# Second attention of a transformer stack: stored relative terms narrowed and stored in two partition halves, split stacks gathered twice

## The reference, cut to what matters

```python
# H = 16 heads, D = 8 channels per head, M = 128, S = 512 tokens, dist_emb has 2*M - 1 = 255 rows
scores = jnp.einsum('bhqd,bhkd->bhqk', q, k)
dist_idx = pos_l - pos_r + M - 1                 # below 0 it wraps, beyond the table it is clipped
pos_emb = dist_emb[dist_idx]
rel_q = jnp.einsum('bhld,lrd->bhlr', q, pos_emb)
rel_k = jnp.einsum('bhrd,lrd->bhlr', k, pos_emb)
probs = jax.nn.softmax((scores + rel_q + rel_k) / sqrt(D), axis=-1)
ctx = jnp.einsum('bhqk,bhkd->bhqd', probs, v)
```

## Time and profile before

| what | us |
|---|---|
| median of 3 runs | 4911.35 |
| profiled execution, its own time | 4912.15 |
| its span in the trace | 4910.4 |
| first phase b1 in the trace, 32 units | 2243 to 3059 |
| second phase b2 in the trace, 32 units | 3059 to 3974 |

### The profile page before, as it was taken

One profiled execution on the slowest core, in us unless ns is written; L12 is line 12 of the kernel. 1 busy time (PEld: TensorE's weight loads), 2 busy tenths in 40 slices (PEclk: granted clock), 3 DMA queues, 4 the chain that ended last, 5 costly groups with the idle time before them and its releaser, 6 DMA issues.

```text
span 4910.4 us, 102424 instructions
## 1 busy us (share of the span) xinstructions
PE 3915.1 (80%) x31924; PEld 2380.9 (48%) x31924; DVE 2889.9 (59%) x6305; ACT 2635.3 (54%) x6550; POOL 1689.6 (34%) x1383
## 2 busy tenths in 40 slices
PE   2999999999488888734666565999999945888886
PEld 1555555554255555522222222677777723555554
DVE  2555555555577777543444443566666665777775
ACT  1555555554367777523333333566666624777774
POOL 0000000000588888523222222111111116878774
PEclk9999999999799999965555555999999977999998
DMA  3222222221111111027999999777777711111111
GB/s 118 87 78 78 78 78 80 81 78 53 49 25 23 27 27 23 17 71 293 380 381 385 380 381 369 269 262 260 248 272 250 256 43 52 25 26 25 25 23 32
DMA packets 374686, 701.06 MB, mean 143 GB/s; under 512 B 54180, under 2 KB 161016, under 8 KB 374568
## 3 DMA queue, kind: packets, MB, share of 16 engines
q1 hardware_dynamic: 330536, 565.25, 33.6%
q0 software_dynamic: 44032, 134.30, 7.4%
HBM read 336.53 MB, written 314.64 MB: 133 GB/s over the span
## 4 chain that ended last, share of the span: by engine, by line
PE 51%; DMA 13%; DVE 10%; issue 9%; POOL 7%; ACT 4%; SPq 2%; DVEq 1%; POOLq 0%; ACTq 0%
DMA rel_k<-b_stage_k 12%; PE ps L332 5%; PE ps L1465 5%; PE ps L340 5%; PE ps L351 5%; PE ps L1474 5%; PE ps L1456 3%; PE ps L1485 3%; DVE f_rs L1028 2%; POOL f_rn L758 2%; PE ps L866 2%; DVE f_rc L1025 2%; POOL f_rot L756 2%; PE ps L1357 2%; DVE b_stage_k L1381 2%
## 5 line engine op out<-in xcount | busy, mean ns | idle before, releaser
L1381 DVE COPY b_stage_k<-ps 128x640 f32<-128x640 f32 (+2 forms) x512 | 359.1, 722 | 469.6 <-DMA rel_k<-b_stage_k 410.3
L430 ACT ACTIVATE a_p<-a_s,a_min 128x512 f32<-128x512 f32 x512 | 366.0, 715 | 470.3 <-DVE a_min L474 470.3
L1378 ACT ACTIVATE b_stage_q<-ps 128x640 f32<-128x640 f32 (+2 forms) x512 | 316.0, 624 | 505.4 <-PE ps L1360 388.0
L474 DVE CUSTOM_DVE_ANT_0 a_s<-ps,a_table 128x512 f32<-128x512 f32 x512 | 333.5, 689 | 374.5 <-PE ps L332 371.9
L1539 ACT ACTIVATE c_p<-c_s,c_min 128x512 f32<-128x512 f32 x512 | 370.2, 723 | 290.7 <-PE ps L1474 180.3
L1357 PE MATMUL ps<-b_e,b_st_k 48*128 48x512 bf16 (+1 forms) x512 | 305.9, 597 | 261.1 <-DVE b_stage_k L1381 261.1
L1574 DVE CUSTOM_DVE_ANT_0 c_s<-ps,c_rq 128x512 f32<-128x512 f32 x512 | 352.8, 689 | 200.8 <-PE ps L1465 188.1
L188 POOL COPY y<-ln_rows 128x512 f32 x32 | 19.9, 621 | 1304.8 <-DVE ln_rows L180 1304.8
L949 ACT ACTIVATE f_p<-f_s,f_min 128x128 f32<-128x128 f32 x1024 | 396.3, 390 | 89.1 <-DVE f_min L1014 88.7
L756 POOL TENSOR_TENSOR f_rot<-f_rc,f_rs 128x1024 f32<-128x1024 f32 x128 | 302.9, 2367 | 255.6 <-DVE f_rs L1028 255.3
L758 POOL TENSOR_TENSOR f_rn<-f_ss,f_power 128x16 f32<-128x16 f32 x128 | 373.8, 2920 | 14.9 <-DVE f_ss L1037 1.4
(11 more groups left out here) (171 smaller groups left out, 9194.5 us busy)
## 6 DMA issues: line engine op xcount, KB each, us to landing
rel_q<-b_stage_q SPq DMA_DIRECT2D x64, 1280.0 KB, 7.8
rel_k<-b_stage_k SPq DMA_DIRECT2D x64, 1280.0 KB, 7.7
c_rq<-rel_q SPq DMA_DIRECT2D x64, 1024.0 KB, 7.7
c_rk<-rel_k POOLq DMA_DIRECT2D x64, 1024.0 KB, 11.9
a_table<-skew_bias SPq DMA_DIRECT2D x64, 896.0 KB, 4.6
f_vb<-f_v SPq DMA_DIRECT2D x256, 128.0 KB, 2.4
rel_k<-b_stage_k SPq DMA_DIRECT2D x32, 1024.0 KB, 9.5
rel_q<-b_stage_q SPq DMA_DIRECT2D x32, 1024.0 KB, 5.3
```

The lines of the kernel that those rows point to most:

```text
L430: nc.scalar.activation(a_p[:, lt % 2, h, :], a_s[:, lt % 2, h, :], ACT.Exp, bias=a_min[:, lt % 2, h:h + 1], scale=-1.0, accum_out=a_sum[:, ...
L1381: moves_b1(dve, 1, lambda out, src: nc.vector.tensor_copy(out, src))
```

## The change

The tensor stack_qk and its stores, waits and semaphore go. The window of q and k loses its last column (and for q's lt 0 the first 127, for k's last lt the last 128), and the columns left out are read in b2 from where the same distance stands 255 columns on, in a second DMA. The window lies at the start of its PSUM banks, so products are split 512 columns after lo. Each store of a slot is split into two DMAs, one of partitions 0 to 63 and one of 64 to 127, each 64 columns narrower than the window. In b2 POOL's queue gathers the stacks from split_qk in 12 DMAs of 32 KB in place of one DMA of 384 KB.

```diff
-    b_st_stored = [starting("b_st_stored0", 32), starting("b_st_stored1", 32)]
     def span(n, t):
-        return (P * max(0, t - 1), WIN) if n == 0 else (0, min(WIN, P * (t + 3)))
+        if n == 0:
+            return (P - 1 if t == 0 else P * (t - 1), WIN - 1)
+        return (0, WIN - 1 - P if t == LT - 1 else min(WIN - 1, P * (t + 3)))
+
+    def reads(n, t):
+        if n == 0:
+            return [(0, P, DIST_B), (P, SEQ, 0)] if t == 0 else [(P * (t - 1), SEQ, 0)]
+        return [(0, SEQ - P, 0), (SEQ - P, SEQ, -DIST_B)] if t == LT - 1 else [(0, min(SEQ, P * (t + 2)), 0)]
...
     def sync_b1(sp):
         def step(u, q, i):
-            hold(sp, b_st_loaded[q], i * 192 + 192)
-            for n in range(2):
-                sp.dma_start(stack_dram[u, n], b_st[n][:, q, :, :]).then_inc(b_st_stored[q], 16)
             for lt in range(LT):
                 for n in range(2):
                     lo, hi = span(n, lt)
                     hold(sp, b_rel_moved[n], u * 16 + (lt * QB + QB + 2))
-                    dst = bass.AP(rel_dram[n].tensor, ..., [[WIN, P], [P * WIN, QB], [1, hi - lo]])
-                    sp.dma_start(dst, b_stage[n][:, lt % 2, :, lo:hi]).then_inc(b_rel_stored[n][lt % 2], 16)
+                    for g in range(2):
+                        f, t = (lo + P // 2, hi) if g == 0 else (lo, hi - P // 2)
+                        dst = bass.AP(rel_dram[n].tensor, ... + (lt * HB * P * WIN + g * (P // 2) * WIN + f),
+                                      [[WIN, P // 2], [P * WIN, QB], [1, t - f]])
+                        sp.dma_start(dst, b_stage[n][g * (P // 2):(g + 1) * (P // 2), lt % 2, :, f:t]
+                                     ).then_inc(b_rel_stored[n][lt % 2], 16)
...
     def tensor_b1(pe):
-                        last = nc.tensor.matmul(ps[:, bank, lo:min(hi, 512)], w, b_e[:, n, at + lo:at + min(hi, 512)],
-                        if hi > 512:
-                            last = nc.tensor.matmul(ps[:, bank + 1, 0:hi - 512], w, b_e[:, n, at + 512:at + hi],
+                        mid = min(hi, lo + SEQ)
+                        last = nc.tensor.matmul(ps[:, bank, 0:mid - lo], w, b_e[:, n, at + lo:at + mid], start=True, stop=True)
+                        if hi > mid:
+                            last = nc.tensor.matmul(ps[:, bank + 1, 0:hi - mid], w, b_e[:, n, at + mid:at + hi],
...
     def pool_b2(pool):
             hold(pool, c_scored, u * TILES + 16)
-            pool.dma_start(c_st[:, q, :, :, :].rearrange("p n h t -> p n (h t)"),
-                           stack_dram[u].rearrange("n p h t -> p n (h t)")).then_inc(c_loaded[q], 16)
+            for n in range(2):
+                for g in range(6):
+                    at = (n * 3 + SPLIT_ORDER[n][g]) * (P * SEQ)
+                    src = bass.AP(split_dram.tensor, ..., [[SEQ, DB], [DB * SEQ, QB], [1, SEQ]])
+                    pool.dma_start(c_st[DB * g:DB * g + DB, q, n, :, :], src).then_inc(c_loaded[q], 16)
             for rt in range(LT):
+                for f, t, by in reads(1, rt):
+                    src = bass.AP(rel_dram[1].tensor, ... + (rt * HB * P * WIN + P - 1 + f + by),
+                                  [[WIN - 1, P], [P * WIN, QB], [1, t - f]])
+                    pool.dma_start(c_rk[:, q, rt, :, f:t], src).then_inc(c_loaded[q], 16)
```

More of the change, by code:

```diff
@@ L1113, in program @@
     split_dram = nc.dram_tensor("split_qk", [BATCH, 2, 3, P, SEQ], BF16).ap()
-    stack_dram = nc.dram_tensor("stack_qk", [UNITS_B, 2, STACK, QB, SEQ], BF16).ap()
     rel_dram = [nc.dram_tensor("rel_q", [BATCH, LT, HB, P, WIN], F32).ap(),
@@ L1297, in program @@
     b_st_loaded = [sem("b_st_loaded0"), sem("b_st_loaded1")]
-    b_st_stored = [starting("b_st_stored0", 32), starting("b_st_stored1", 32)]
     b_rel_full = [starting("b_relq_full", 32), starting("b_relk_full", 32)]
     b_rel_moved = [starting("b_relq_moved", 2), starting("b_relk_moved", 2)]
-    b_rel_stored = [[starting("b_relq_stored0", 16), starting("b_relq_stored1", 16)],
-                    [starting("b_relk_stored0", 16), starting("b_relk_stored1", 16)]]
+    b_rel_stored = [[starting("b_relq_stored0", 32), starting("b_relq_stored1", 32)],
+                    [starting("b_relk_stored0", 32), starting("b_relk_stored1", 32)]]
     def span(n, t):
-        return (P * max(0, t - 1), WIN) if n == 0 else (0, min(WIN, P * (t + 3)))
+        if n == 0:
[5 more added lines that the diff above has]
+        return [(0, SEQ - P, 0), (SEQ - P, SEQ, -DIST_B)] if t == LT - 1 else [(0, min(SEQ, P * (t + 2)), 0)]
     def unit_loop(eng, step):
@@ L1315, in step @@
         def step(u, q, i):
-            hold(pool, b_st_stored[q], i * 32 + 32)
             hold(pool, b_rel_full[0], u * 16 + 16)
@@ L1335, in step @@
                     hold(sp, b_rel_moved[n], u * 16 + (lt * QB + QB + 2))
-                    dst = bass.AP(rel_dram[n].tensor,
-                                  (u // QB) * (LT * HB * P * WIN) + (u % QB) * (QB * P * WIN) + (lt * HB * P * WIN + lo),
-                                  [[WIN, P], [P * WIN, QB], [1, hi - lo]])
-                    sp.dma_start(dst, b_stage[n][:, lt % 2, :, lo:hi]).then_inc(b_rel_stored[n][lt % 2], 16)
+                    for g in range(2):
+                        f, t = (lo + P // 2, hi) if g == 0 else (lo, hi - P // 2)
+                        dst = bass.AP(rel_dram[n].tensor, (u // QB) * (LT * HB * P * WIN) + (u % QB) * (QB * P * WIN)
+                                      + (lt * HB * P * WIN + g * (P // 2) * WIN + f), [[WIN, P // 2], [P * WIN, QB], [1, t - f]])
+                        sp.dma_start(dst, b_stage[n][g * (P // 2):(g + 1) * (P // 2), lt % 2, :, f:t]
+                                     ).then_inc(b_rel_stored[n][lt % 2], 16)
         unit_loop(sp, step)
         for n in range(2):
-            sp.wait_ge(b_st_stored[n], 32 + 32 * (UNITS_B // 2))
             for q in range(2):
-                sp.wait_ge(b_rel_stored[n][q], 16 + 16 * (UNITS_B * 2))
+                sp.wait_ge(b_rel_stored[n][q], 32 + 32 * (UNITS_B * 2))
     def tensor_b1(pe):
@@ L1356, in step @@
                         lo, hi = span(n, lt)
-                        last = nc.tensor.matmul(ps[:, bank, lo:min(hi, 512)], w, b_e[:, n, at + lo:at + min(hi, 512)],
-                                                start=True, stop=True)
-                        if hi > 512:
-                            last = nc.tensor.matmul(ps[:, bank + 1, 0:hi - 512], w, b_e[:, n, at + 512:at + hi],
+                        mid = min(hi, lo + SEQ)
+                        last = nc.tensor.matmul(ps[:, bank, 0:mid - lo], w, b_e[:, n, at + lo:at + mid], start=True, stop=True)
+                        if hi > mid:
+                            last = nc.tensor.matmul(ps[:, bank + 1, 0:hi - mid], w, b_e[:, n, at + mid:at + hi],
                                                     start=True, stop=True)
@@ L1367, in step @@
             for lt in range(LT):
-                eng.wait_ge(b_rel_stored[n][lt % 2], u * 32 + (16 * (lt // 2) + 16))
+                eng.wait_ge(b_rel_stored[n][lt % 2], u * 64 + (32 * (lt // 2) + 32))
                 for h in range(QB):
@@ L1372, in step @@
                     lo, hi = span(n, lt)
-                    move(b_stage[n][:, lt % 2, h, lo:hi], ps[:, bank:bank + 2, :].rearrange("p b n -> p (b n)")[:, lo:hi])\
+                    move(b_stage[n][:, lt % 2, h, lo:hi], ps[:, bank:bank + 2, :].rearrange("p b n -> p (b n)")[:, 0:hi - lo])\
                         .then_inc(b_rel_moved[n], 1)
@@ L1424, in step @@
             hold(pool, c_scored, u * TILES + 16)
-            pool.dma_start(c_st[:, q, :, :, :].rearrange("p n h t -> p n (h t)"),
-                           stack_dram[u].rearrange("n p h t -> p n (h t)")).then_inc(c_loaded[q], 16)
+            for n in range(2):
+                for g in range(6):
+                    at = (n * 3 + SPLIT_ORDER[n][g]) * (P * SEQ)
+                    src = bass.AP(split_dram.tensor, (u // QB) * (6 * P * SEQ) + (u % QB) * (QB * DB * SEQ) + at,
+                                  [[SEQ, DB], [DB * SEQ, QB], [1, SEQ]])
+                    pool.dma_start(c_st[DB * g:DB * g + DB, q, n, :, :], src).then_inc(c_loaded[q], 16)
             for rt in range(LT):
-                src = bass.AP(rel_dram[1].tensor, (u // QB) * (LT * HB * P * WIN) + (u % QB) * (QB * P * WIN)
-                              + (rt * HB * P * WIN + P - 1), [[WIN - 1, P], [P * WIN, QB], [1, min(SEQ, P * (rt + 2))]])
-                pool.dma_start(c_rk[:, q, rt, :, 0:min(SEQ, P * (rt + 2))], src).then_inc(c_loaded[q], 16)
+                for f, t, by in reads(1, rt):
+                    src = bass.AP(rel_dram[1].tensor, (u // QB) * (LT * HB * P * WIN) + (u % QB) * (QB * P * WIN)
+                                  + (rt * HB * P * WIN + P - 1 + f + by), [[WIN - 1, P], [P * WIN, QB], [1, t - f]])
+                    pool.dma_start(c_rk[:, q, rt, :, f:t], src).then_inc(c_loaded[q], 16)
             hold(pool, c_pv, u * LT + 4)
@@ L1440, in step @@
```

(12 more changed lines are left out.)

## The result

The changed kernel takes 4994.79 us (median of 4 runs, 4991.87 to 5000.06), the kernel before in the same comparison 4910.84 us: 1.0173 times as long, 95% interval 1.0155 to 1.0191. Slower was right, but 84 us were lost where 276 were forecast. Rival B, partial overlap at 5018 us, came nearest.

A forecast was written before the change was run, and what follows sets the result against it. Full DMA engines were taken to bound the first phase, PE the second. Stores 33.0 + gathers 1.1 = 34.1 us per unit, 275 us more over 32 units; 4912 + 275 + 1 = 5188 us, range 4740 to 5290.

The forecast's parts named there:

- Rival B: First phase: the halves' stores overlap in part, 265 GB/s, 3.3 us more per unit, kernel 5018 us; chance 0.14.
- What bounds the kernel: First phase: DMA engines are full, 25.5 us per unit, no compute engine near its bound; second phase: PE, 27.9 us.
- The stack's stores, 2.1 us per unit: First phase: dropping these stores saves 2.1 us per unit, 67 us over 32, with nothing taking their place there.
- Narrower windows at full rate: First phase: fewer columns, 7.33 MB with the halves' cuts, would take 18.0 us in place of 21.8 at 408 GB/s.
- The split: First phase: stores from half the partitions move at 222 GB/s, between 214 and 231, so 33.0 us per unit.
- My reason against overlap: First phase: engines running ahead wait at the slot for the same new DMA and start level again; no size given.
- The rule of the Trainium skill: First phase: each half reaches 8 of 16 ports, two concurrent DMAs gain only 6%: 34.9 us stores, kernel about 5249 us.
- Issues on SP at no cost: First phase: 16 DMAs per unit in place of 10 cost nothing while transfers last over 25 us.
- Odd edges at nothing: First phase: store rows off round addresses cost nothing; from the other side 10% would be 3 us per unit.
- The second phase: Twelve gathers on POOL cost the steady state nothing, cover 5.8 us; the start costs 1 us, between 0 and 6.5.
- What would show it: Signs: first phase some 1090 us at about 225 GB/s, DMA share 1.0; second phase's steady unit stays at 27.9 us.
- The range: Whole kernel: 4740 to 5290 us, widened from 5120 to 5300 to leave out no more than 2 in 10.

## Why the prediction was right in sign and wrong in size

- *What bounds the kernel:* right. The first phase followed the transfers in every experiment but the one with smaller DMAs, where SP was the bound. (The page shows six slices at 9 tenths or more, not seven; nothing rests on it.)
- *The stack's stores, 2.1 us per unit:* right in kind; alone their going gave 59 us with 67 counted.
- *Narrower windows at full rate:* right. The model 20.5 + 1.1 + 0.75 gave 22.4 us per unit, 22.5 measured.
- *The split, "I take 222 GB/s":* this is the step that failed. The mechanism was right: one-sided stores alone go at 209 GB/s, inside the rows' 198 to 214. The term is mis-sized because opposite neighbours overlap more than I allowed. 7.33 MB took 26.8 us, 273 GB/s, where 33.0 us stood in the sum; times 32 that is 198 us too much. 214 came from transfers to and from partitions 0 to 47 alone, 231 from such stores among stores of all 128 partitions: neither had a store of the other half alone beside it, so they could not price what the change does. My reason against overlap, that engines level at the slot, was not seen in numbers; against stores of one side only, taking sides in turn saves 267 us, and 98 of these go when two of one side follow each other. With B's 265 GB/s, set down as a rival, the sum is 5018 us. B was the only rival with partial overlap, but its 265 was taken from no row either: that it came within 8 GB/s is luck.
- *The rule of the Trainium skill ("SBUF — State Buffer", Door 1: The DMA port swizzle):* it gives partitions 0 to 63 half of the ports, and 209 GB/s against 408 agree with that. The 6% that the same page of the Trainium skill gives, in the section "Can I just issue two DMAs to hit both halves?", for two DMAs to both halves does not hold for a full queue of alternating stores: 31% here, and 4995 us measured against the prediction's estimate of 5249 us by that 6%.
- *Issues on SP at no cost:* right for 16 DMAs (the cut by heads); with 32 SP became the bound.
- *Odd edges at nothing:* right (4995.62 against 4994.79).
- *The second phase:* its steady state costs nothing, as said, and POOL's wait for c_pv is gone. The start was put at 1 us between 0 and 6.5; it is 4.0. rel_k's loads leave 6.7 us later, and not all of it reaches PE.
- *What would show it:* 225 GB/s at a share of 1.0 was announced, 277 at 0.93 came.
- *The range:* 4740 to 5290 us holds the measured time because it reaches from one rival nearly to the other. That says nothing for the sum inside it.

## What to carry to other kernels

Before a DMA is cut to save bytes, ask whether each piece still reaches all 128 partitions: here a cut by heads was free and a cut by partitions of the same bytes cost 203 us. A trace that already holds a narrow transfer shows its rate, in single microseconds with the DMA share near 1 and the GB/s halved; but a rate read from one transfer says nothing on how neighbours of opposite sides overlap, and that needs its own case. A change of several parts can hide a gain in a loss: the stacks alone gave 1.2%, whole narrowed stores with them 1.8 to 2.0%.

## What the runs showed of the hardware

- One-sided stores in a full queue: 209 GB/s; sides in turn, one queue: 273 GB/s with rows of 1.3 to 2.3 KB. With the gathers counted in, that is 278 GB/s; 307 with rows of 1.5 to 2.6 KB, 360 with rows of 2.56 KB that adjoin in DRAM, and 253 with the short rows and two DMAs of one side at a time.
- SP's issue of a store from 64 partitions takes at least 0.60 us, from 128 partitions at least 0.37 us, with 256 rows in each. The rows don't set it: 128 rows from 64 partitions (the smaller DMAs) take 0.60 us as well, and 512 rows from 128 (the kernel before) 0.37 us. The two lines are of the changed kernel and of the cut by heads (min/median/max ns):

```profile
...
L1342 SPq DMA_DIRECT2D rel_q<-b_stage_q x256: 602/1332/2447, 2248.6 to 3125.7; - x128
...
```

```profile
...
L1341 SPq DMA_DIRECT2D rel_q<-b_stage_q x256: 372/372/1082, 2247.7 to 2954.8; - x128
...
```

- The median of 1332 ns is SP held up by its queue: at half the speed of transfer, with one side only, it is 2054 ns. So SP leading the chain of waits did not make SP the bound; the cut by heads, with as many issues, tells the two apart.
